# Graph network layer on one core: the forward transform of each 64-time tile as products of their own, instead of one product against a table with zeros

## The chip, the cores and the metric

One NeuronCore of one Trainium2 chip (eight cores) runs the whole kernel as one launch. The metric is the time of one execution on the device in microseconds. Lower is better.

## The reference, cut to what matters

There are 64 graphs of 256 nodes with 256 features, all in fp32. Two layers run one after the other, each as x + layer(relu(layernorm(x))). Layer 0 is a normalised adjacency product and a linear map. Layer 1 takes, for each graph, the 256 nodes also as a sequence of 256 times:

```python
xc = jnp.transpose(x, (0, 2, 1))
h = _bn(_conv1d(xc, conv1_w, 0), bn1_g, bn1_b, bn1_m, bn1_v)      # 256 -> 256, one tap
h = jax.nn.relu(h)
h = _bn(_conv1d(h, conv2_w, 8), bn2_g, bn2_b, bn2_m, bn2_v)       # 256 -> 256, 17 taps
x_conv = jnp.transpose(jax.nn.relu(h + xc), (0, 2, 1))
...
A = jnp.exp(-dist) * mask
x_nmp = jnp.einsum('bnm,bmd->bnd', A, msg)
x_in = jnp.concatenate([x_conv, x_nmp], axis=-1)
gi = x_in @ w_ih.T + b_ih
gh = x @ w_hh.T + b_hh
```

and a gated update (sigmoid, sigmoid, tanh) behind it. The change concerns the convolution with 17 taps, which the kernel does with discrete Fourier transforms.

## The kernel before, in words

The kernel has three stages. The **first stage** is a software pipeline over the 64 graphs, one turn per graph and eleven more turns to drain. Each engine has its own function (`first_scalar`, `first_vector`, `first_gpsimd`, `first_tensor`, `first_sync`) with a hand-written order of steps, and each step works on the graph that is some turns behind (`live(i, lag)` gives b = i - lag). Semaphores join the engines, and every engine executes its own list strictly in the order written. The **second stage** goes over 40 frequencies: 256x256 complex products of spectra and filter spectra. The filter spectra come from `filter_unit` (L706, lhsT of 119 rows and for the last part 68 rows). The **third stage** goes over pairs of graphs: the inverse transform (L1019) and the gates.

TensorE's turn in the first stage is, in the order of `first_tensor`: `out0` (12 products of 256 columns with split operands, through the helper `multiply` at L113), `nmp` (12 more), `agg` (L615: four fp32 products of 256 columns), `dist` (L624: two), `s` (6 through L113), the **forward transform** (L644), `cm1` and `cm0` (12 of 512 columns through L113), and four transposes (L663). An fp32 product with fp32 operands shows in the trace as two weight loads and two matmuls. A product with operands of the rounded type fp32r (all of L113, L624) shows as one of each.

The forward transform cuts the 256 times of a graph into four tiles of 64, zero-padded to NT = 80. Two tiles lie above each other on the 128 partitions of `h1[b % 2][:, n, :]`: tile t of half n on rows 64t to 64t + 63. The table `ft` is 128 x 160. Its rows 0 to 63 hold the 80 cosines and sines in columns 0 to 79 and zeros in the rest, and its rows 64 to 127 hold zeros in columns 0 to 79 and the same 80 in columns 80 to 159. So one product with all 128 rows gives both tiles' spectra side by side. Per graph there are four such products, for channel half c and node half n; c = 0 goes to PSUM bank `DFT`, c = 1 to bank `OUT0`, which the graph's `out0` also uses. That is why the c = 1 half waits for `u` (L641): VectorE's step at L473 reads `OUT0` in the same turn.

ScalarE copies each bank to the staging tile `xst` in `spectrum_out` (L324, called at L379 and L386 with the cast `axh`, L384, between the calls); it signals `xe0` and `xe1`. `store_spectra` (L277 to L283) sends each quarter of a group of four graphs out on SP's queue. Other steps that the text speaks of: ScalarE's `msh` (L345), which waits for `nmp` of TensorE, its `xt` (L408) and `xxh` (L339), with which its own turn ends and the next begins; VectorE's `xxl` (L439), which waits for `xxh`, then `uvh` (L444), `uv` (L448), `ah` (L458), and `u` (L473).

Of the kernel before, what the change touches and what calls it, by code (L numbers as in the profile page):

```python
# [14 lines left out]
NT = 80  # L15
NF = NT // 2
TILE = 64
# [83 lines left out]
def mm3(lhs, rhs, o, first, last, pairs):  # L101

    n = 3 * len(pairs)
    i = 0
    for l, r in pairs:
        for a, c in ((0, 0), (0, 1), (1, 0)):
            yield lhs[a][l], rhs[c][r], o, first and i == 0, last and i == n - 1
            i += 1


def multiply(e, steps):
    for l, r, o, start, stop in steps:
        done = e.matmul(o, l, r, start=start, stop=stop, skip_group_check=True)  # L113
    return done
# [14 lines left out]
def gnn_kernel(nc, x, adj, adjt, w0t, w1mt, wset, wgt, w2r, bc, cols, ftab, gtab, ttab, eye, out):  # L129
    NB = x.shape[0]  # L130
# [19 lines left out]
    with ExitStack() as ctx:  # L150
        S = {n: ctx.enter_context(nc.semaphore(n)) for n in NAMES}
        P = [ctx.enter_context(nc.psum_tensor(f"P{i}", [128, 512], F32)) for i in range(8)]
# [23 lines left out]
        ft = p1("ft", [128, 2 * NT])  # L176
# [40 lines left out]
        h1 = [p1(f"h1{i}", [128, 2, 256]) for i in range(2)]  # L217
        af = p1("af", [128, 512])
        xst = [p1(f"xst{i}", [128, 2, NT, 16]) for i in range(2)]
# [27 lines left out]
        DFT, OUT0, NMP, DIST, AG, SXN, CM1, CM0 = range(8)  # L247
# [11 lines left out]
        def live(i, lag, n=NB):  # L259
            return 0 <= i - lag < n  # L260
# [16 lines left out]
        def store_spectra(e, k):  # L277

            g, c, r = k // 4, k % 2, k % 4 // 2
            e.wait_ge(S[f"xe{c}"], 4 * g + 4)  # L280
            e.e.dma_start(xh_d[:, c, r * NF // 4:(r + 1) * NF // 4, g, :],
                          xst[g % 2][:, c, r * NF:(r + 1) * NF, :].rearrange("p (q s) t -> p q (s t)", s=4)).then_inc(
                              S[f"sx{'ab'[r]}{g % 2}"], 16)  # L283

        def first_sync(e, i):
            if live(i, 0):
                if i + 1 < NB:
                    load_x(e, i + 1)
                    load_adj(e, i + 1)
                load_adjt(e, i)  # L290

            if live(i, 11, NB - 4):
                store_spectra(e, i - 11)
            if NB + 7 <= i < NB + 9:
                for n in range(2):
                    store_spectra(e, NB - 4 + 2 * (i - NB - 7) + n)
            if live(i, 8):
                b = i - 8
                e.wait_ge(S["nm"], b + 1)
                e.e.dma_start(nm_d[b], nm[:, :]).then_inc(S["snm"], 16)  # L300
            if live(i, 4):
                b = i - 4
                e.wait_ge(S["x2"], b + 1)
                e.e.dma_start(x2_d[b].rearrange("(t p) c -> p t c", p=128), x2[b % 2][:, :, :]).then_inc(S[f"sx2{b % 2}"], 16)
            if live(i, 5):
                b = i - 5
                e.wait_ge(S["xt"], b + 1)
                e.e.dma_start(xn_d[b // 2][:, :, b % 2, :],
                              xt[:, :].rearrange("p (c t) -> p c t", c=2)).then_inc(S["sxt"], 16)
            if live(i, 8, NW):  # L310
                j = i - 8
                n = 17 * parts(j)
                e.wait_ge(S["taps"], j - 1)
                e.e.dma_start(taps[0:n, j, :], w2r[119 * j:119 * j + n]).then_inc(S[f"tap{j % 2}"], 16)

        def spectrum_out(e, b, c):

            g, j = b // 4, b % 4
            src = P[(DFT, OUT0)[c]][:, 0:4 * NT].rearrange("p (j r) -> p r j", j=4)
            dst = xst[g % 2][:, c, :, 4 * j:4 * j + 4]  # L320
            e.wait_ge(S[f"dft{c}"], b + 1)
            for half in "ab":
                e.wait_ge(S[f"sx{half}{g % 2}"], 32 * (g // 2))
            e.e.copy(dst, src).then_inc(S[f"xe{c}"], 1)  # L324

        def relu(e, b):
            e.wait_ge(S["tcm0"], b + 1)
# [4 lines left out]
        def first_scalar(e, i):  # L332
# [45 lines left out]
            if live(i, 7):  # L378
                spectrum_out(e, i - 7, 0)  # L379
# [5 lines left out]
            if live(i, 7):  # L385
                spectrum_out(e, i - 7, 1)  # L386
# [193 lines left out]
        def first_tensor(e, i):  # L580
            if live(i, 3):
                b = i - 3
# [5 lines left out]
                for n in range(2):  # L588
                    t = multiply(e.e, mm3([{f: h[:, f * 256 + n * 128:f * 256 + n * 128 + 128] for f in range(2)}
                                           for h in ag],  # L590
                                          [{f: h[:, f, :] for f in range(2)} for h in w0],
                                          P[OUT0][:, n * 256:n * 256 + 256], True, True, [(0, 0), (1, 1)]))
                t.then_inc(S["out0"], 1)
            if live(i, 7):
                b = i - 7
# [5 lines left out]
                for d in range(2):  # L601
                    t = multiply(e.e, mm3([{m: h[:, m, d * 128:d * 128 + 128] for m in range(2)} for h in ms],
                                          [{m: h[:, m * 256:m * 256 + 256] for m in range(2)} for h in ax],
                                          P[NMP][:, d * 256:d * 256 + 256], True, True, [(0, 0), (1, 1)]))
# [3 lines left out]
            if live(i, 2):  # L608
                b = i - 2
# [3 lines left out]
                for f in range(2):  # L613
                    for m in range(2):
                        t = e.e.matmul(P[AG][:, f * 256:f * 256 + 256], hd[b % 2][:, m, f * 128:f * 128 + 128],  # L615
                                       ah[b % 2][:, m * 256:m * 256 + 256], start=m == 0, stop=m == 1,
                                       skip_group_check=True)
                t.then_inc(S["agg"], 1)
            if live(i, 6):
                b = i - 6  # L620
                e.wait_ge(S["uv"], b + 1)
                e.wait_ge(S["af"], b)
                for m in range(2):
                    t = e.e.matmul(P[DIST][:, m * 256:m * 256 + 256], uv[0:96, 0, m * 128:m * 128 + 128],  # L624
                                   uv[0:96, 1, :], start=True, stop=True, skip_group_check=True)
                t.then_inc(S["dist"], 1)
            if live(i, 5):
                b = i - 5
# [6 lines left out]
            if live(i, 7):  # L635
                b = i - 7
                e.wait_ge(S["h1"], b + 1)
                e.wait_ge(S["ft_in"], 16)
                for c, k in ((0, DFT), (1, OUT0)):
                    if c == 1:  # L640
                        e.wait_ge(S["u"], min(b + 5, NB))  # L641
                    e.wait_ge(S[f"xe{c}"], b)
                    for n in range(2):
                        t = e.e.matmul(P[k][:, n * 2 * NT:n * 2 * NT + 2 * NT], h1[b % 2][:, n, c * 128:c * 128 + 128],  # L644
                                       ft[:, :], start=True, stop=True, skip_group_check=True)
                    t.then_inc(S[f"dft{c}"], 1)
            if live(i, 5):
                b = i - 5
                for k, n, name, freed in ((CM1, 1, "cm1", "tcm1"), (CM0, 0, "cm0", "tcm0")):
# [5 lines left out]
            if live(i, 4):  # L655
                b = i - 4
# [4 lines left out]
                for c in range(2):  # L661
                    for n in range(2):
                        t = e.e.transpose(P[SXN][:, c * 256 + n * 128:c * 256 + n * 128 + 128],  # L663
                                          xn[:, n, c * 128:c * 128 + 128], ident[:, :])
# [818 lines left out]
        def _(tensor):  # L1483
# [5 lines left out]
            for i in range(4):  # L1489
                first_tensor(e, i)  # L1490
# [5 lines left out]
            for n in range(2):  # L1496
                t = tensor.matmul(P[CM0][:, n * 128:n * 128 + 128], ones[:, :], diag[:, 4 + n, :],
                                  start=True, stop=True, skip_group_check=True)
            t.then_inc(S["rows"], 1)
            first_tensor(e, 4)  # L1500
            e.wait_ge(S["normrow"], 2)
            for i in range(5, TURNS):
                first_tensor(e, i)
# [62 lines left out]
```

## Time and profile before

| | |
|---|---|
| median of 3 runs | 1789.55 us (1788.72 to 1789.57) |
| profiled execution | 1790.36 us |
| its span, first to last instruction | 1788.6 us |
| TensorE's granted clock, mean over the span | 0.998 |
| first stage | about 0 to 660 us |

The profile is one execution, recorded by the hardware. "Busy" of TensorE is modelled from start times and sizes, so that the distance between two starts (the pitch) says more than a duration does. PE is TensorE's matmul side, PEld its weight loads, DVE VectorE, ACT ScalarE, POOL GpSimd, SP the engine that issues DMAs. A merged row ("x8") spans from the first start to the last end of that many equal instructions in a row.

### The profile page before, as it was taken

Reading aid. Unit: us, or ns where it says so; the run is one execution under the profiler, and the core shown is the slowest. Engines: PE = TensorE matmul, PEld = TensorE weight load, DVE = VectorE, ACT = ScalarE, POOL = GpSimd, SP = SyncE. Lnnn points to the kernel's source line nnn. Section 1 sums busy time; section 2 is a strip of 40 time slices with the busy share of each in tenths; the row PEclk is TensorE's granted clock in tenths of the full one; section 3 lists DMA queues with packets and bytes.
Section 4 is the critical chain, followed back from the end, with each engine's and each line's share of the span. In section 5 each row is a group of like instructions: output and inputs, shape, how many; then the busy total and the mean of one; then the engine's idle time right before and its main releaser. Section 6 shows DMA issues by size and latency. Waiting matters only on the chain.

```text
span 1788.6 us, 29955 instructions
## 1 busy us (share of the span) xinstructions
PE 1774.4 (99%) x10266; PEld 1574.9 (88%) x10266; DVE 1212.5 (68%) x2318; ACT 997.3 (56%) x1787; POOL 830.7 (46%) x991
## 2 busy tenths in 40 slices
PE   8999999999999999999999999999999999999998
PEld 7999999999999999999988888888888888888887
DVE  8999999999999847665664454554554544545545
ACT  5888888888888876665743233233332332332322
POOL 5788888887777627655722122221221221212211
PEclk9999999999999999999999999999999999999999
DMA  6566666676656554544762534534435345344342
GB/s 214 179 201 210 206 207 209 201 214 191 209 184 202 144 163 148 179 161 171 245 189 73 123 79 108 116 78 116 93 97 120 79 107 116 81 115 101 91 111 42
DMA packets 511381, 262.56 MB, mean 147 GB/s; under 512 B 366215, under 2 KB 474119, under 8 KB 511230
## 3 DMA queue, kind: packets, MB, share of 16 engines
q1 hardware_dynamic: 510686, 260.58, 52.3%
q8 instruction: 83, 1.36, 0.3%
q14 instruction: 68, 0.56, 0.1%
q10 hardware_dynamic: 544, 0.07, 0.0%
HBM read 151.51 MB, written 109.05 MB: 146 GB/s over the span
## 4 chain that ended last, share of the span: by engine, by line
PE 97%; issue 1%; POOL 1%; DVE 0%; ACT 0%; DMA 0%; SPq 0%; POOLq 0%; ACTq 0%; DVEq 0%
PE P L113 72%; PE P L615 6%; PE P L1019 5%; PE P L874 4%; PE P L644 4%; PE P L706 3%; PE P L663 1%; PE P L624 1%; PE P L1488 1%; DMA tt_w<-in_ttab 0%; POOL axl L578 0%; POOL af L575 0%; ACT xn L354 0%; DVE wh0l L837 0%; DVE x L473 0%
## 5 line engine op out<-in xcount | busy, mean ns | idle before, releaser
L1001 POOL TENSOR_TENSOR xnx1l<-xnf,xnx1h 128x1024 fp32r<-128x1024 f32 x16 | 44.2, 2761 | 336.2 <-ACT xnx1h L994 336.2
L1001 POOL TENSOR_TENSOR xnx0l<-xnf,xnx0h 128x1024 fp32r<-128x1024 f32 x15 | 41.6, 2774 | 317.1 <-ACT xnx0h L994 317.1
L1124 ACT ACTIVATE tr<-P,cold 128x512 f32<-128x512 f32 x64 | 44.2, 690 | 192.3 <-PE P L113 192.3
L1127 ACT ACTIVATE nn<-gn,col 128x512 f32<-128x512 f32 x64 | 46.4, 724 | 182.3 <-DVE gn L1148 182.3
L1157 DVE SCALAR_TENSOR_TENSOR tz<-tz,tr 128x512 f32<-128x512 f32 x63 | 43.6, 692 | 142.5 <-ACT tz L1138 142.5
L1138 ACT ACTIVATE tz<-P,cold 128x512 f32<-128x512 f32 x63 | 43.4, 688 | 156.8 <-PE P L113 156.8
L1144 DVE SCALAR_TENSOR_TENSOR gn<-tr,gn 128x512 f32<-128x512 f32 x64 | 45.0, 703 | 125.9 <-ACT tr L1124 125.9
L575 POOL TENSOR_TENSOR af<-af,at 128x512 f32<-128x512 f32 x64 | 110.1, 1720 | 42.8 <-ACT af L366 40.5
L578 POOL TENSOR_TENSOR axl<-af,axh 128x512 fp32r<-128x512 f32 x64 | 101.2, 1582 | 55.6 <-ACT axh L384 55.6
L615 PE MATMUL P<-ah,hd 128*128 128x256 f32 x512 | 121.4, 380 | 0.0
L113 PE MATMUL P<-w1mh,xxh 128*128 128x512 f32 x256 | 107.9, 422 | 0.0
L1019 PEld LDWEIGHTS P<-gt,yt 128*128 128x128 f32 x768 | 98.9, 190 | 4.9
L615 PEld LDWEIGHTS P<-ah,hd 128*128 128x128 f32 x512 | 93.2, 191 | 10.0
L113 PE MATMUL P<-w1mh,xxl 128*128 128x512 f32 x256 | 101.2, 395 | 0.0
L113 PE MATMUL P<-w1ml,xxh 128*128 128x512 f32 x256 | 101.1, 395 | 0.0
L1019 PE MATMUL P<-gt,yt 128*128 128x136 f32 (+1 forms) x768 | 100.8, 281 | 0.0
L498 DVE SCALAR_TENSOR_TENSOR x<-x,x 128x512 f32<-128x512 f32 x64 | 99.8, 1559 | 0.1
L899 DVE TENSOR_TENSOR yo<-P,mt 128x512 f32<-128x512 f32 x78 | 53.5, 686 | 66.5 <-PE P L113 66.5
L1148 DVE TENSOR_TENSOR gn<-gn,P 128x512 f32<-128x512 f32 x64 | 44.0, 688 | 66.9 <-PE P L113 66.9
L706 PE MATMUL P<-tt_w,taps 119*128 119x140 f32 (+1 forms) x592 | 80.8, 283 | 0.0
L113 PE MATMUL P<-w0h,agh 128*128 128x256 f32 x256 | 77.5, 303 | 3.2 <-DVE w0l L463 2.1
L726 ACT COPY wf<-P 128x420 f32<-128x420 f32 (+1 forms) x94 | 46.8, 512 | 60.1 <-PE P L706 59.9
(215 smaller groups left out, 6423.0 us busy)
## 6 DMA issues: line engine op xcount, KB each, us to landing
xh_d<-xst SPq DMA_DIRECT2D x64, 320.0 KB, 4.6
y_d<-yo SPq DMA_DIRECT2D x80, 256.0 KB, 2.2
xl<-xh_d SPq DMA_DIRECT2D x36, 512.0 KB, 4.5
x<-in_x SPq DMA_DIRECT2D x64, 256.0 KB, 2.7
a<-in_adj SPq DMA_DIRECT2D x64, 256.0 KB, 3.1
at<-in_adjt SPq DMA_DIRECT2D x64, 256.0 KB, 3.9
x_d<-x SPq DMA_DIRECT2D x64, 256.0 KB, 4.2
xn_d<-xt SPq DMA_DIRECT2D x64, 256.0 KB, 4.0
```

The lines of the kernel that those rows point to most:

```text
L113: done = e.matmul(o, l, r, start=start, stop=stop, skip_group_check=True)
L498: e.e.scalar_tensor_tensor(out=o[:, :, :], in0=o[:, :, :], scalar=0.0, in1=xs[b % 5][:, :, :], op0=ALU.max, op1=ALU.add).then_inc(S["x2"], 1)
L575: e.e.tensor_tensor(af[:, :], af[:, :], at[b % 7][:, :], ALU.mult).then_inc(S["am"], 1)
L578: e.e.tensor_tensor(ax[1][:, :], af[:, :], ax[0][:, :], ALU.subtract).then_inc(S["axlo"], 1)
L615: t = e.e.matmul(P[AG][:, f * 256:f * 256 + 256], hd[b % 2][:, m, f * 128:f * 128 + 128], ah[b % 2][:, m * 256:m * 256 + 256], start=m == ...
L644: t = e.e.matmul(P[k][:, n * 2 * NT:n * 2 * NT + 2 * NT], h1[b % 2][:, n, c * 128:c * 128 + 128], ft[:, :], start=True, stop=True, skip_gr ...
L706: t = e.e.matmul(P[k][:, m * 140:m * 140 + 140], taps[0:n_rows, j0 + m, c * 128:c * 128 + 128], tt_w[0:n_rows, part * 140:part * 140 + 140 ...
L726: e.e.copy(dst, src).then_inc(S["wev"], 1)
L874: t = e.e.matmul(common(chunk)[:, 0:256], xsum[f % 3][:, c, 128 * chunk:128 * chunk + 128], wsum[f % 3][:, c, :], start=c == 0, stop=c == ...
L899: e.e.tensor_tensor(yo[n % 4][:, :].rearrange("p (q o) -> p q o", q=2), main(chunk)[:, :].rearrange("p (q o) -> p q o", q=2), mt[chunk][:, ...
L1001: e.e.tensor_tensor(o[1][:, :, :], xnf[p % 2][:, :, :, :].rearrange("p c i t -> p c (i t)"), o[0][:, :, :], ALU.subtract).then_inc(done, 1)
L1019: t = e.e.matmul(P[k][:, o * 256 + first:o * 256 + end], y[:, j, o * 128:o * 128 + 128], gt[:, g:g + end - first], start=o == 0 and j == 0 ...
```

## The change

The transform is issued as eight products of 64 rows and 80 columns rather than four of 128 rows and 160 columns. Tile t reads rows 64t to 64t + 63 of `h1` and of `ft`, and writes to a bank that belongs to the tile (t = 0 to `DFT`, t = 1 to `OUT0`) where before the bank belonged to the channel half. The two tiles' products alternate. All waits (for `u`, for both `xe`) now stand ahead of the first product, and both banks are signalled at the end. `spectrum_out` and `store_spectra` follow: a copy takes one tile's spectra of both channel halves and writes every other element of four, and a store waits for both copies. The table `ft` is not changed.

```diff
         def store_spectra(e, k):
 
             g, c, r = k // 4, k % 2, k % 4 // 2
-            e.wait_ge(S[f"xe{c}"], 4 * g + 4)
+            for t in range(2):
+                e.wait_ge(S[f"xe{t}"], 4 * g + 4)
...
-        def spectrum_out(e, b, c):
+        def spectrum_out(e, b, t):
 
             g, j = b // 4, b % 4
-            src = P[(DFT, OUT0)[c]][:, 0:4 * NT].rearrange("p (j r) -> p r j", j=4)
-            dst = xst[g % 2][:, c, :, 4 * j:4 * j + 4]
-            e.wait_ge(S[f"dft{c}"], b + 1)
+            src = P[(DFT, OUT0)[t]][:, 0:4 * NT].rearrange("p (c n r) -> p c r n", c=2, n=2)
+            dst = xst[g % 2][:, :, :, 4 * j + t:4 * j + 4:2]
+            e.wait_ge(S[f"dft{t}"], b + 1)
             for half in "ab":
                 e.wait_ge(S[f"sx{half}{g % 2}"], 32 * (g // 2))
-            e.e.copy(dst, src).then_inc(S[f"xe{c}"], 1)
+            e.e.copy(dst, src).then_inc(S[f"xe{t}"], 1)
...
                 b = i - 7
                 e.wait_ge(S["h1"], b + 1)
                 e.wait_ge(S["ft_in"], 16)
-                for c, k in ((0, DFT), (1, OUT0)):
-                    if c == 1:
-                        e.wait_ge(S["u"], min(b + 5, NB))
-                    e.wait_ge(S[f"xe{c}"], b)
+                e.wait_ge(S["u"], min(b + 5, NB))
+
+                for t in range(2):
+                    e.wait_ge(S[f"xe{t}"], b)
+                for c in range(2):
                     for n in range(2):
-                        t = e.e.matmul(P[k][:, n * 2 * NT:n * 2 * NT + 2 * NT], h1[b % 2][:, n, c * 128:c * 128 + 128],
-                                       ft[:, :], start=True, stop=True, skip_group_check=True)
-                    t.then_inc(S[f"dft{c}"], 1)
+                        for t, k in ((0, DFT), (1, OUT0)):
+                            at_ = (2 * c + n) * NT
+                            rows = slice(TILE * t, TILE * t + TILE)
+                            d = e.e.matmul(P[k][:, at_:at_ + NT], h1[b % 2][rows, n, c * 128:c * 128 + 128],
+                                           ft[rows, NT * t:NT * t + NT], start=True, stop=True, skip_group_check=True)
+                            if c == 1 and n == 1:
+                                d.then_inc(S[f"dft{t}"], 1)
```

## Rows read from the trace of the kernel before

**Rows 1.** The page: busy time by engine, TensorE's clock, the chain that ended last.

```profile
PE 1774.4 (99%) x10266; PEld 1574.9 (88%) x10266; DVE 1212.5 (68%) x2318; ACT 997.3 (56%) x1787; POOL 830.7 (46%) x991
...
PEclk9999999999999999999999999999999999999999
...
PE 97%; issue 1%; POOL 1%; DVE 0%; ACT 0%; DMA 0%; SPq 0%; POOLq 0%; ACTq 0%; DVEq 0%
```

**Rows 2.** Windows, the steady first stage, one turn: us, then PE, PEld, DVE, ACT, POOL busy.

```profile
402.02:411.85 9.83, 9.83 (x67) 9.03 (x65) 9.57 (x24) 8.63 (x18) 7.99 (x14) 1.00 0.75 242
```

**Rows 3.** Timeline of PE in one turn: start us, us, engine, line, operation, out<-in, count.

```profile
400.27 0.28 PE L113 MATMUL P<-axh,msl 128*128 128x256 f32 x1
400.39 1.89 PE L615 MATMUL P<-ah,hd 128*128 128x256 f32 x8
...
402.94 0.28 PE L113 MATMUL P<-xxh,wsel 128*128 128x256 f32 x1
403.06 1.25 PE L644 MATMUL P<-ft,h 128*128 128x160 f32 x8
404.04 0.50 PE L113 MATMUL P<-w1mh,xxh 128*128 128x512 f32 x1
404.38 0.39 PE L113 MATMUL P<-w1ml,xxh 128*128 128x512 f32 x1
404.61 0.39 PE L113 MATMUL P<-w1mh,xxl 128*128 128x512 f32 x1
```

**Rows 4.** The line L644: durations in ns (min/median/max), first and last start.

```profile
L644 PE MATMUL P<-ft,h x512: 297/299/302, 49.2 to 659.8; 128*128 128x160 f32 x171
```

**Rows 5.** Timelines of PE and PEld, the shortest fp32 products (128 columns, ahead of the pipeline).

```profile
18.65 1.05 PE L1493 MATMUL P<-diag,ones 128*128 128x128 f32 x8
...
19.43 0.53 PEld L1497 LDWEIGHTS P<-diag,ones 128*128 128x128 f32 x4
```

**Rows 6.** Lines L1488 and L1497: 128 columns at the low clock and at the full one.

```profile
L1488 PEld LDWEIGHTS P<-ones x52: 191/333/337, 1.1 to 9.7; 128*128 128x128 f32 x52
L1488 PE MATMUL P<-ones x52: 274/421/584, 1.1 to 9.8; 128*128 128x128 f32 x52
...
L1497 PEld LDWEIGHTS P<-diag,ones x4: 192/192/193, 19.4 to 19.8; 128*128 128x128 f32 x4
L1497 PE MATMUL P<-diag,ones x4: 275/276/276, 19.5 to 19.9; 128*128 128x128 f32 x4
```

**Rows 7.** Groups by line and shape, weight loads of L706: count, busy us, mean ns.

```profile
L706 PEld LDWEIGHTS P<-tt_w,taps 119*128 119x128 f32 x576 | 73.4, 190 | 0.1
...
L706 PEld LDWEIGHTS P<-tt_w,taps 68*128 68x128 f32 x16 | 2.5, 192 | 0.0
```

**Rows 8.** Timeline of PEld, the transposes of one turn, and the line L663 in ns.

```profile
34.46 0.59 PEld L663 LDWEIGHTS P<-ident,xn 128*128 128x128 f32 x4
...
L663 PEld LDWEIGHTS P<-ident,xn x256: 137/141/144, 24.5 to 641.1; 128*128 128x128 f32 x128
```

**Rows 9.** Timelines of PEld and PE where TensorE starts again after a wait.

```profile
31.09 0.19 PEld L113 LDWEIGHTS P<-xxh,wseh 128*128 128x128 f32 x1 [2.11 <-ACT xxh L339]
...
31.32 0.28 PE L113 MATMUL P<-xxl,wseh 128*128 128x256 f32 x1
31.43 0.28 PE L113 MATMUL P<-xxh,wsel 128*128 128x256 f32 x1
```

**Rows 10.** Timelines of DVE and ACT in the turn of rows 3.

```profile
399.64 0.69 DVE L439 TENSOR_TENSOR xxl<-P,xxh 128x512 fp32r<-128x512 f32 x1 [0.21 <-ACT xxh L339]
...
402.09 0.87 DVE L473 SCALAR_TENSOR_TENSOR x<-P,sm,b 128x256 f32<-128x256 f32 x2
...
400.67 0.63 ACT L345 ACTIVATE msh<-tcm 128x512 fp32r<-128x512 f32 x1 [1.06 <-PE P L113]
...
404.93 0.43 ACT L324 COPY xst<-P 128x320 f32<-128x320 f32 x1
...
408.82 0.62 ACT L339 CAST xxh<-xt 128x512 fp32r<-128x512 f32 x1
```

**Rows 11.** Waits of SP's queue up to 700 us: us in total, times, longest.

```profile
SPq L98 <- DVE x L498: 189.5, 59, 6.5
...
SPq L281 <- ACT xst L324: 9.0, 3, 5.7
```

## The prediction

> **What bounds the kernel now.** First the page: TensorE is busy 99% of the span at the full clock, and 97% of the chain that ended last is its own work [rows 1]. So the question is which stretch the change touches and whether TensorE is dense there. The windows answer it: one turn of the first stage lasts 9.83 us, TensorE fills all of it, VectorE 9.57, ScalarE 8.63, GpSimd 7.99 [rows 2]. TensorE is the bound, and VectorE stands only 9.83 - 9.57 = 0.26 us behind it. Time added to TensorE's turn is added to the kernel 64 times; time taken from it comes back only as far as VectorE and the waits between the engines let it.
>
> The timeline gives the price of the transform now. Its eight matmuls span 1.25 us, the last lasting 0.299 [rows 3, 4], so the pitch is (1.25 - 0.30) / 7 = 0.136 us, and the block costs 8 x 0.136 = 1.09 us of a turn: from 403.06 to 404.15, where the next block's first product must have begun (404.38 less one pitch of 0.23). For 160 columns of fp32 that is near 2 cycles a column at 2.4 GHz, 0.133 us. This block is bound by the moving columns; its loads hide beneath them.
>
> **The change part by part.** It removes 8 matmuls of 160 columns and 8 loads a turn and issues 16 of each, with 80 columns. The moving columns are halved product by product: 0.136 / 2 = 0.068 us for each, 16 x 0.068 = 1.09 us, as much as before. Nothing is won by that unless the two halves of the array work at the same time.
>
> *The loads.* There are now twice as many, each still of 128 columns. Does a load of 64 rows cost less? L706 loads 68 rows in 192 ns and 119 rows in 190 [rows 7]: rows don't matter there. How short can the pitch of an fp32 load be? A load's record has a fixed part, but between the low clock (1.2 GHz) and the full one its median falls by 333 - 192 = 141 ns, and that of a matmul with 128 columns by 421 - 276 = 145 ns [rows 6]. So a load seems to occupy its path about as long as 128 moving columns occupy theirs. The pitch of such products is (1.05 - 0.275) / 7 = 0.111 us, that of their loads (0.53 - 0.192) / 3 = 0.113 us [rows 5]. I take 0.112. One after another, 16 loads cost 16 x 0.112 = 1.79 us, which is 0.70 us more than the 1.09 of now. Over 64 turns: +45 us. The bounds for this term: below, the loads hide (pitch 0.068, +0 us); above, the pitch of the transposes, (0.59 - 0.141) / 3 = 0.150 us [rows 8], with 0.141 for one load, the median of that line, thus 16 x 0.150 = 2.40, +84 us. I take 0.112, because it is of the same type and columns as the new loads.
>
> *Do the tiles overlap?* No row of this trace has products on part of the rows, so it can't say. The order within a pair speaks against it: each fp32 product is load, matmul, load, matmul on one tile, and the other tile's pair follows. In rows 3 and 5 loads and matmuls go in the order written, with a load one place ahead. If that order also holds between tiles, the four loads of a pair stay in a line, and nothing overlaps. That is my forecast.
>
> *The change of mode.* A turn goes from products of all rows to products of half, and back. No row shows the price of that. Below it is 0. Above: the next load may not start before the last matmul has left. Where TensorE starts after a wait, the load begins at 31.09 and the first matmul takes effect at 31.32 - 0.11 = 31.21 [rows 9]: 0.11 us that are hidden elsewhere. The last matmul's own tail, 0.28 - 0.12 = 0.16 us [rows 3], comes on top: 0.27 us a switch. I take 0.11 a switch, since a load that loses its cover is the least that a separation of the two kinds costs, 0.22 us a turn, 64 x 0.22 = +14 us; bounds 0 and +35. The Trainium skill, "TensorEngine Tiling (Array Packing)", Key Properties, says that changing the tiling mode drains TensorE, while staying in a mode and changing the tile doesn't. By that rule the switch would cost the tail too, +35 us in place of +14; no row here can show it.
>
> *The waits.* The wait for `u` moves from the middle of the block to its front. `u` ends at 402.96 [rows 10], and TensorE reaches the block at 402.94 with its load and at 403.06 with its matmul [rows 3]: on the edge. VectorE's chain to `u` hangs on `xxh` (402.96 is 3.32 behind the start of `xxl` at 399.64), and `xxh` on a ScalarE turn of 8.8 us that starts with `msh`, when TensorE's `nmp` is done [rows 10]. From that `nmp` to the next block TensorE has its whole turn with one transform in it. So if the transform grows, `u` is early by just that much and the wait costs nothing; queued behind it are `cm1`, `cm0`, the transposes and the next `out0`, none of which then waits. If it shrinks by g, `u` comes when it came, and the loop nmp, msh, xxh, u, transform, nmp covers two turns with only one transform shortened: half of g is given back.
>
> *The copies.* Both banks are signalled at the end of the block. ScalarE asks for the first at 404.93 [rows 10], 4.26 us behind `msh`. The old block's results are out at about 404.3. The new block ends 0.7 to 1.2 us later, so ScalarE stands still for up to 0.6 us. It has 1.06 us of idle time a turn, and the turn itself grows; `axh`, `h`, `nm`, `hd`, `xt` and `xxh` are queued behind it and slip by that much inside a longer turn. Cost 0. If the turn did not grow, this slip would reach `xxh` and `xxl`, which VectorE awaits already (0.21) [rows 10]. The copy keeps its 320 elements; bounds for the new stride are 0 and a copy twice as long, 2 x 0.43 us a turn, under ScalarE's 1.06; I take 0. SP's store waits for one semaphore more, but stores are issued a turn or more behind the copies, and SP spends 190 us waiting for `x2` anyway [rows 11]; cost 0, and at the end of the stage its wait is for the second copy already.
>
> **The sum.** 45 + 14 = +59 us. The profiled execution took 1790.36 us, 0.81 above the median of 1789.55; against it the changed kernel takes 1849.4, against the median 1848.6. I say **1849 us**. The forecast's own range is 1789.55 + 45 = 1835 to 1789.55 + 45 + 35 = 1870, with the slower load pitch a little more.
>
> **The rivals.** What a measurement can tell from no change is 0.2%, 3.6 us.
>
> *Both tiles work at once and the switch is cheap (ends faster).* Tile 1's loads and matmuls run beside tile 0's, so the block is eight steps of 0.112, the load still the slower part: 0.90 us, g = 0.19. The wait for `u` gives back half: 64 x 0.095 = 6 us, 1783. If the wait costs nothing, 64 x 0.19 = 12, 1777. It decides from the point at which the two switches together cost less than 0.19 us. For it: halves of different partitions share no rows. Against it: the order of the loads. The Trainium skill, "TensorE: Matmul & The Clock Gate", Part 3, says that products in distinct row groups run concurrently and that a load is pulled ahead when its row group differs from those in flight. This rival is what follows from it here.
>
> *Both at once, but each switch costs.* The block is 0.90 + 0.22 to 0.90 + 0.54 = 1.12 to 1.44 us, that is +2 to +22 us; middle +12, 1802.
>
> *Loads never bound, tiles in a line.* The block stays at 16 x 0.068 = 1.09 and the switches are free: 1790, the same. Against it stand the equal clock steps of rows 6.
>
> *Both at once and loads hidden as well.* Eight steps of 0.068 make 0.54, g = 0.55; half of it, 0.27, meets VectorE's 0.26: 64 x 0.26 = 17 us, 1773.
>
> **How the numbers follow.** Forecast 0.52, the pair with switch costs 0.18, the pair without 0.17, loads never bound 0.08, everything hidden 0.05. Faster: 0.17 + 0.05 = 0.22. Same: 0.08 + 0.02 of the second = 0.10. Slower: 0.52 + 0.16 = 0.68. For 8 in 10 the range must reach past 1783, the middle of the faster rival, and up to 1872; it leaves out the best case, half of the faster rival and a little above. It is wide since cases of both signs are open; the likeliest one's own range is 1835 to 1872.
>
> **What would show it.** In the changed trace L644's successor lines should have 16 records of each kind a turn, with starts 0.11 us apart, a block of about 2.0 us, and a turn of about 10.75 us with VectorE still at 9.6. Starts of the two tiles' matmuls within a few ns of each other would prove overlap and the forecast wrong. A block under 0.9 us with TensorE idle ahead of it, released by L473, would be the rival of the `u` wait. Gaps of over 0.1 us in front of and behind the block measure the switch. Behind 660 us nothing should change.

## The result and the profile after

The changed kernel takes 1799.91 us (median of 4 runs, 1799.2 to 1800.46) against 1789.56 us before: ratio 1.0058, 95% interval 1.0045 to 1.0071. It is 10.4 us slower. The prediction had the direction, but said 1849: its +59 us is nearly six times too much, so its account of the change was wrong. What came is one of its rivals: the two tiles work at the same time, and each change of mode is paid (+2 to +22 us, 1802, chance 0.18). A change of mode is here the step from products of all the rows to products of half of them, or back.

The windows of the changed kernel, for one steady turn; columns as in [rows 2]:

```profile
402.78:412.78 10.00, 10.00 (x75) 8.98 (x73) 9.58 (x24) 8.68 (x18) 7.87 (x14) 1.00 0.67 203
```

A turn takes 10.00 us in place of 9.83, TensorE still fills it, and the others have hardly changed. 64 x 0.17 = 10.9 us: the whole loss lies in these turns. The first and the last start of the transform say the same, 620.8 us apart (L649 below) in place of 610.6 [rows 4]. Behind the last transform the kernel before needs 1788.6 - 659.8 = 1128.8 us [rows 4] and the changed one 1797.9 - 668.9 = 1129.0.

TensorE's timeline in that turn, then the loads' (PEld), against [rows 3]:

```profile
407.70 0.27 PE L113 MATMUL P<-xxh,wsel 128*128 128x256 f32 x1
407.90 1.12 PE L649 MATMUL P<-ft,h 64*128 64x80 f32 x16
408.95 0.50 PE L113 MATMUL P<-w1mh,xxh 128*128 128x512 f32 x1
409.30 0.40 PE L113 MATMUL P<-w1ml,xxh 128*128 128x512 f32 x1
...
407.59 0.19 PEld L113 LDWEIGHTS P<-xxh,wsel 128*128 128x128 f32 x1
407.90 0.97 PEld L649 LDWEIGHTS P<-ft,h 64*128 64x128 f32 x16
408.95 0.19 PEld L113 LDWEIGHTS P<-w1mh,xxh 128*128 128x128 f32 x1
```

Sixteen matmuls span 1.12 us, less than the 1.25 us of the eight before. In a line at 0.112 us they would have spanned 15 x 0.112 + 0.27 = 1.95. They ran in twos. Cut to a short window, the timeline shows the first two loads together in 0.19 us, while the line's shortest load is 0.182 (third row below): the two starts are under 0.02 us apart. The first two matmuls together take 0.34, and the longest one of the line 0.334. In the trace's records the two tiles' starts are 6 to 7 ns apart.

```profile
407.90 0.19 PEld L649 LDWEIGHTS P<-ft,h 64*128 64x128 f32 x2
407.90 0.34 PE L649 MATMUL P<-ft,h 64*128 64x80 f32 x2
...
L649 PEld LDWEIGHTS P<-ft,h x1024: 182/188/188, 48.1 to 668.8; 64*128 64x128 f32 x171
L649 PE MATMUL P<-ft,h x1024: 272/272/334, 48.1 to 668.9; 64*128 64x80 f32 x171
```

The step between twos comes from the loads: (0.97 - 0.19) / 7 = 0.111 us. Eight steps are 0.89 us, 0.20 less than the old block's 1.09.

The block as a whole is nevertheless longer. By the prediction's own reckoning it lasts from 407.70 + 0.12 = 407.82 to 409.30 - 0.23 = 409.07, that is 1.25 us. So 1.25 - 0.89 = 0.36 us lie at its ends. In front, the first load starts 0.20 us behind the last matmul of the products before it (407.90 against 407.70). Behind, the last matmul starts at 409.02 - 0.27 = 408.75, and the next load at 408.95, again 0.20 us later. In the kernel before, load and matmul start together at both ends: at 402.94 in front (the matmul in [rows 3]), and behind at 404.01, where the last matmul starts at 403.06 + 1.25 - 0.30 = 404.01. Its loads:

```profile
402.94 1.12 PEld L644 LDWEIGHTS P<-ft,h 128*128 128x128 f32 x8
404.01 0.19 PEld L113 LDWEIGHTS P<-w1mh,xxh 128*128 128x128 f32 x1
```

The account that the experiments test is **+0.36 us a turn for two changes of mode, -0.20 for the overlap, 64 x 0.16 = +10.2 us**.

On the other engines, the chain that might have bound does not:

```profile
404.27 0.69 DVE L440 TENSOR_TENSOR xxl<-P,xxh 128x512 fp32r<-128x512 f32 x1 [0.38 <-ACT xxh L340]
...
406.72 0.87 DVE L474 SCALAR_TENSOR_TENSOR x<-P,sm,b 128x256 f32<-128x256 f32 x2
...
L325 ACT COPY xst<-P x128: 430/444/453, 49.8 to 669.5; 128x320 f32<-128x320 f32 x128
```

VectorE's idle time grows from 0.21 to 0.38 us. `u` ends at 407.59, 0.31 us ahead of the first load. The copies with the new stride take 444 ns (424 before), and all but two, in the last turns, find their bank ready.

### The profile page after: what moved, and what is told of

Same layout as the page of the kernel before. It is cut to its first block, busy times and chain, and to the rows that moved or that the text cites. A ratio compares the mean times of both kernels' runs of the same rounds, so it can differ in the third digit from the quotient of the medians.

```text
span 1797.9 us, 30995 instructions
## 1 busy us (share of the span) xinstructions
PE 1782.9 (99%) x10778; PEld 1568.7 (87%) x10778; DVE 1211.1 (67%) x2318; ACT 999.6 (56%) x1787; POOL 823.8 (46%) x991
## 4 chain that ended last, share of the span: by engine, by line
PE 96%; DVE 1%; issue 1%; POOL 1%; ACT 0%; DMA 0%; POOLq 0%; ACTq 0%; DVEq 0%
PE P L113 72%; PE P L616 6%; PE P L1025 5%; PE P L880 4%; PE P L649 4%; PE P L712 3%; PE P L669 1%; PE P L625 1%; POOL axl L579 0%; POOL af L576 0%; DMA x<-in_x 0%; DVE sm L487 0%; DVE sm L493 0%; DVE agl L421 0%; DVE x L474 0%
## 5 line engine op out<-in xcount | busy, mean ns | idle before, releaser
L576 POOL TENSOR_TENSOR af<-af,at 128x512 f32<-128x512 f32 x64 | 102.5, 1602 | 50.8 <-ACT af L367 50.7
L579 POOL TENSOR_TENSOR axl<-af,axh 128x512 fp32r<-128x512 f32 x64 | 92.1, 1439 | 64.7 <-ACT axh L385 64.7
L346 ACT ACTIVATE msh<-tcm 128x512 fp32r<-128x512 f32 x64 | 40.3, 630 | 77.5 <-PE P L113 77.0
```

Of the source, the lines that this page charges most:

```text
L576: e.e.tensor_tensor(af[:, :], af[:, :], at[b % 7][:, :], ALU.mult).then_inc(S["am"], 1)
L579: e.e.tensor_tensor(ax[1][:, :], af[:, :], ax[0][:, :], ALU.subtract).then_inc(S["axlo"], 1)
```

## The experiments

All ratios are to the kernel before, on the same chip. It took 1789.2 to 1789.5 us beside them and 1789.6 beside the changed kernel, so a difference to the changed kernel's 1799.91 holds to about 0.4 us.

### Is the gap in front a wait? (kernel before, waits moved)

```diff
+                e.wait_ge(S["u"], min(b + 5, NB))
+                for c in range(2):
+                    e.wait_ge(S[f"xe{c}"], b)
                 for c, k in ((0, DFT), (1, OUT0)):
-                    if c == 1:
-                        e.wait_ge(S["u"], min(b + 5, NB))
-                    e.wait_ge(S[f"xe{c}"], b)
```

> The kernel before, with the waits for u and both xe moved to the front of the transform, products unchanged. Theory A (the 10.4 us come from two changes of mode a turn, 0.15 us in front and 0.20 behind, less 0.19 gained by overlap): 1789.6 us, within 2 us of before. Rival B (the gap in front of the block is the moved wait for u, not the mode): 64 x 0.15 = +10 us, 1799.

Measured: 1792.38 us, ratio 1.0015 (1.0006 to 1.0024), +2.9 us. Theory A's bound of 2 us is missed by a little, rival B's +10 by far. The line's row shows what the edge costs:

```profile
L644 PE MATMUL P<-ft,h x512: 297/299/375, 48.6 to 661.8; 128*128 128x160 f32 x171
```

The first and last starts are 613.2 us apart, before 610.6 [rows 4]: 0.04 us a turn on the mean of 63, in which the load waits for `u`. The prediction had called this "on the edge". In the changed kernel the turn is 0.17 us longer, and `u` ends 0.11 us ahead of the last matmul in front of the block (407.59 against 407.70), so nothing of it remains there.

### What do the loads cost in a line? (changed kernel, all rows)

```diff
-                            d = e.e.matmul(P[k][:, at_:at_ + NT], h1[b % 2][rows, n, c * 128:c * 128 + 128],
-                                           ft[rows, NT * t:NT * t + NT], start=True, stop=True, skip_group_check=True)
+                            d = e.e.matmul(P[k][:, at_:at_ + NT], h1[b % 2][:, n, c * 128:c * 128 + 128],
+                                           ft[:, NT * t:NT * t + NT], start=True, stop=True, skip_group_check=True)
```

> The changed kernel, but each of the eight products of 80 columns uses all 128 rows (the zeros of the table take the other tile out), so there is no mode and no overlap. Theory A: 16 loads in a line at 0.112 us, no switch: 1.79 against 1.09 us a turn, +0.70 x 64 = +45 us over before, 1834. Rival C (loads of 128 columns take less than 0.068 us and hide; the 0.112 us steps of the changed kernel are something of the row tiles): 1790.

Measured: 1837.12 us, ratio 1.0265 (1.0249 to 1.0281), +47.6 us. Its transform, in the timeline of PE:

```profile
408.54 1.98 PE L649 MATMUL P<-ft,h 128*128 128x80 f32 x16
```

The pitch is (1.98 - 0.275) / 15 = 0.114 us. Rival C falls. The price of a load in the prediction was right, and this kernel is what the prediction took the changed one to be, without the modes: it costs the +45 us that stand there and 2.6 more.

The 2.6 come from `u`, nearly all. In every second turn (28 of 64) the first load waits for it and starts 0.14 us behind the matmul in front; in the others, with the same waits in the same place, load and matmul start together. So it is not the place of the waits that makes the gap of 0.20 us in the changed kernel. In one late turn `u` ends at 407.57 + 0.86 = 408.43 and the load starts at 408.50, where the matmul started at 408.36. The block's first matmul then starts at 408.54 in place of 408.36 + 0.12 = 408.48 and lasts 0.307 us in place of 0.275: 28 x 0.09 = 2.5 us. The lateness comes from an engine that bounds nothing: ScalarE's `axh` had waited 0.73 us for GpSimd's `af`, and `xxh`, `xxl` and `u` come after it.

```profile
401.00 0.62 ACT L385 CAST axh<-af 128x512 fp32r<-128x512 f32 x1 [0.73 <-POOL af L576]
...
407.57 0.86 DVE L474 SCALAR_TENSOR_TENSOR x<-P,sm,b 128x256 f32<-128x256 f32 x2
...
408.50 1.86 PEld L649 LDWEIGHTS P<-ft,h 128*128 128x128 f32 x16
```

### How far ahead are the tiles taken up? (tiles in a line, tiles by twos)

```diff
-                for c in range(2):
-                    for n in range(2):
-                        for t, k in ((0, DFT), (1, OUT0)):
+                for t, k in ((0, DFT), (1, OUT0)):
+                    for c in range(2):
+                        for n in range(2):
```

> The changed kernel with the loops exchanged: all four products of tile 0, then all four of tile 1. Theory A with a short look ahead (the overlap needs the tiles side by side in the program): 16 steps of 0.112 and two switches of 0.35 together, 2.14 against 1.09 us, +67 us over before, 1857. Rival D (the engine looks far enough ahead to take tile 1's loads and products while tile 0's run): 1800, as the changed kernel. Something between the two measures how far it looks.

Measured: 1831.21 us, ratio 1.0234 (1.022 to 1.0248), +41.7 us. It falls between the two theories. The loads in the timeline, whole and cut at 407.46:

```profile
406.93 1.48 PEld L649 LDWEIGHTS P<-ft,h 64*128 64x128 f32 x16
...
406.93 0.70 PEld L649 LDWEIGHTS P<-ft,h 64*128 64x128 f32 x6
```

All sixteen take (1.48 - 0.19) / 0.111 = 11.6 steps, where a line would take 15 and twos 7. Tile 0's first five loads start 0.11 us apart; the sixth of the second row starts at 0.70 - 0.18 = 0.52 us, ahead of the 0.55 at which tile 0's sixth is due. It is tile 1's first. When it starts, three of tile 0's eight are still to come. The records of the matmuls that carry the tiles' signals agree: tile 0's last starts at 407.78, tile 1's at 408.29, 0.51 us later, where the changed kernel has under 0.01 us between the two. So the engine takes up work of the free tile past loads and matmuls that wait for the busy one, in this order only some three of each far. The section on the kernel before says that every engine executes its list strictly in the order written. Between two tiles TensorE does not.

For the second order only the two inner loops are exchanged, so that the tile changes after every second product:

```diff
-                    for n in range(2):
-                        for t, k in ((0, DFT), (1, OUT0)):
+                    for t, k in ((0, DFT), (1, OUT0)):
+                        for n in range(2):
```

> The changed kernel with the tiles alternating after every second product (four loads and matmuls) rather than after every one. In the run with the tiles in line, tile 1's first load started beside tile 0's fifth matmul, with three left. Theory A with that look ahead (three loads and matmuls): tile 1 starts one or two steps of 0.112 late and the rest overlaps, +0.11 to 0.22 us a turn, +7 to +14 over the changed kernel, 1807 to 1814. Rival D (the look ahead counts more): 1800.

Measured: 1802.72 us, ratio 1.0076 (1.0059 to 1.0093), 2.8 us above the changed kernel. Between the theories again, and nearer to D: its sixteen loads span 1.03 us against 0.97, half a step late, not one or two. Four loads and matmuls of one tile in a row are nearly covered, eight are not.

```profile
409.62 1.03 PEld L649 LDWEIGHTS P<-ft,h 64*128 64x128 f32 x16
```

### What does a change of mode cost? (four changes, with a control)

```diff
                 for c in range(2):
+                    if c == 1 and live(i, 5):
+                        e.wait_ge(S["tcm1"], i - 5)
+                        multiply(e.e, cm_steps(1, CM1)[0:1])
                     for n in range(2):
```

This is the first product of `cm1`, which is left out behind the transform.

> The changed kernel with the first product of cm1 (all rows) moved into the middle of the transform, between channel halves, so that a turn has four changes of mode and the same work. Theory A: another 0.35 us a turn over 62 turns, +22 us over the changed kernel, 1822. Rival B (the gaps at the block's ends are waits, and a change of mode is free): 1800.

> Control for the run with four changes of mode: the same move of cm1's first product into the middle of the transform, made in the kernel before, where all products use all rows. Theory A: no mode, no cost, 1789 to 1791. If the move itself costs (the changed order, the wait for tcm1, the switch between fp32 and fp32r), up to the 21 us that it added to the changed kernel, 1810.

Measured: 1821.25 us with the changed kernel's products (ratio 1.0177, 1.0163 to 1.0191), which is 21.3 over the changed kernel, and 1789.63 us with those of the kernel before (1.0001, 0.9992 to 1.001). The same move costs nothing where all products use all rows, and 21.3 / 62 = 0.34 us a turn where it adds two changes of mode. Rival B falls. The timeline of PE with four changes:

```profile
400.15 0.27 PE L113 MATMUL P<-xxh,wsel 128*128 128x256 f32 x1
400.35 0.68 PE L657 MATMUL P<-ft,h 64*128 64x80 f32 x8
400.96 0.50 PE L113 MATMUL P<-w1mh,xxh 128*128 128x512 f32 x1
401.39 0.68 PE L657 MATMUL P<-ft,h 64*128 64x80 f32 x8
401.99 0.50 PE L113 MATMUL P<-w1ml,xxh 128*128 128x512 f32 x1
```

The 0.20 us between 400.15 and 400.35 is the gap in front that the changed kernel has, and there is one at each change (400.35 + 0.68 - 0.27 = 400.76 to 400.96, for one).

Fewer rows alone do not make the gap. `dist` uses 96 of the 128 rows, between products of all 128. In the kernel before its second matmul starts at 401.93 + 0.59 - 0.28 = 402.24, and so does the next load:

```profile
401.93 0.59 PE L624 MATMUL P<-uv 96*128 96x256 f32 x2
...
402.24 0.19 PEld L113 LDWEIGHTS P<-xxh,wseh 128*128 128x128 f32 x1
```

### Once a visit, or by the product? (one product split; the block three times)

In the kernel with the waits in front, one product of four is issued as two tiles, from the second graph on; its second half goes to the other bank, so these 80 spectra are stale.

```diff
                     for n in range(2):
+                        if c == 0 and n == 0 and b:
+                            for j, half_out in ((0, P[DFT]), (1, P[OUT0])):
+                                rows = slice(TILE * j, TILE * j + TILE)
+                                e.e.matmul(half_out[:, NT * j:NT * j + NT], h1[b % 2][rows, n, c * 128:c * 128 + 128],
+                                           ft[rows, NT * j:NT * j + NT], start=True, stop=True, skip_group_check=True)
+                            continue
```

> The kernel before with the waits in front (which took 1792.4), and one of its four products, the first, issued as the two 64-row products; its second tile goes to the other bank and is overwritten, so that part of the spectra is stale. Theory A: 0.35 us for the changes of mode, two steps of 0.112, three products of 0.272 left: 1.39 against 1.09 us, +0.30 x 63 = +19 over 1790, less what the moved wait costs, 1809. Rival G (a change of mode costs in proportion to the products in it): a quarter of the changed kernel's 10 us, 1793 to 1795.

Measured: 1807.96 us, ratio 1.0104 (1.0089 to 1.0119), +18.8 us. Splitting one product costs more than splitting all four: the change is paid once a visit, that is once for all the products between two changes of mode, and each split product earns a little back (two steps of 0.112 in place of 0.272 us). Rival G falls.

```profile
401.85 0.27 PE L113 MATMUL P<-xxh,wsel 128*128 128x256 f32 x1
402.05 0.45 PE L647 MATMUL P<-ft,h 64*128 64x80 f32 x4
402.43 1.08 PE L650 MATMUL P<-ft,h 128*128 128x160 f32 x6
```

Then the whole block three times in one visit, and as its measure the same in the kernel before:

```diff
-                for c in range(2):
+                for c in (0, 1, 0, 1, 0, 1):
...
-                    for n in range(2):
+                    for n in (0, 1, 0, 1, 0, 1):
```

The first of the two edits is to the changed kernel, where both banks are signalled after the last pair; the second is to the kernel before.

> The changed kernel with its whole block of products issued three times in a row (the same values to the same places), in one visit to the mode. Theory A: sixteen more steps of 0.112 us a turn, 1.79 x 64 = +115 us over the changed kernel, 1915. If the ends of the block cost in proportion to its products rather than once a visit: three times the block of 1.25 us, +160 us, 1960.

> The kernel before with its four products issued three times. Both theories: sixteen more steps of 0.136 us, 2.17 x 64 = +139 us, 1928. Theory A then has the run with the changed kernel's block three times 13 to 14 us below this one: with enough products in one visit the tiles win. If the ends cost in proportion, this one stays the faster by about 31 us.

Measured: 1913.84 us (1.0695, 1.0678 to 1.0713) and 1927.44 us (1.077, 1.0754 to 1.0787). The tiles now win by 13.6 us, as theory A has it: 64 x (0.36 - 3 x 0.20) = -15 us by the rounded terms. The loads of the one and the matmuls of the other:

```profile
401.48 2.76 PEld L650 LDWEIGHTS P<-ft,h 64*128 64x128 f32 x48
```

```profile
407.90 3.42 PE L644 MATMUL P<-ft,h 128*128 128x160 f32 x24
```

24 steps of (2.76 - 0.19) / 23 = 0.112 us stand against 24 of (3.42 - 0.30) / 23 = 0.136.

### What sets the step? (wider products, one tile)

```diff
-                            at_ = (2 * c + n) * NT
+                            at_ = (2 * c + n) * 128
...
-                            ... P[k][:, at_:at_ + NT] ... ft[rows, NT * t:NT * t + NT]
+                            ... P[k][:, at_:at_ + 128] ... ft[rows, 32 * t:32 * t + 128]
```

The 48 columns more are zeros of the table, and ScalarE's copy (`spectrum_out`) still takes the 80 that count.

> The changed kernel with 128 moving columns a product instead of 80 (the 48 more are zeros of the table, and land in unused columns of the banks). Theory A (the step of 0.112 us is the weight load's, and the moving columns hide below it as long as 2 cycles a column stay under it, 128 x 2 / 2.4 = 0.107 us): 1800, as the changed kernel, within 3 us. Rival E (the moving columns count in the step, or the end of the block): 8 x 0.04 us a turn, +20 us, 1820.

Measured: 1802.35 us, ratio 1.0073 (1.0058 to 1.0088), 2.4 us above the changed kernel. The loads take what they took:

```profile
409.29 0.97 PEld L649 LDWEIGHTS P<-ft,h 64*128 64x128 f32 x16
```

With 48 columns more the step stays at 0.111 us, so the load sets it. 2.4 / 64 = 0.04 us a turn is what 48 columns cost once (48 x 0.136 / 160 = 0.04): the sixteen matmuls span 1.16 us in place of 1.12. Rival E charged this in all eight steps and was right for one.

```profile
409.30 1.16 PE L649 MATMUL P<-ft,h 64*128 64x128 f32 x16
```

Last, three of tile 1's four products are left out (most of its spectra stay stale):

```diff
-                        for t, k in ((0, DFT), (1, OUT0)):
+                        for t, k in ((0, DFT), (1, OUT0))[0:2 if c == 1 and n == 1 else 1]:
```

> The changed kernel with three of tile 1's four products left out, so that most of the second tile's spectra are stale. Theory A (the second tile runs wholly beside the first and costs nothing): the same block, 1800, within 2 us. Rival F (the two tiles share something, for one the path of the loads): less by up to the three products' share, 6 x 0.056 us a turn, -21 us, 1779.

Measured: 1799.58 us, ratio 1.0057 (1.0042 to 1.0072), 0.3 us under the changed kernel. Its ten loads take 0.96 us, the sixteen of the changed kernel 0.97:

```profile
408.02 0.96 PEld L649 LDWEIGHTS P<-ft,h 64*128 64x128 f32 x10
```

The second tile costs nothing, loads included. Rival F falls.

## Why the prediction was wrong

*What bounds the kernel*: right. The loss is TensorE's turn, 64 times, and the time behind the last transform is the same within 0.2 us.

*The loads' price*: right in itself. 0.112 us was taken from products of the same kind; 0.114 was measured in a line, 0.111 in pairs. That rows don't matter was right too. The upper bound of 0.150 was misread: in the trace the four loads of [rows 8] start at 34.46, 34.70, 34.80 and 34.91, so one of them waits behind a matmul of 512 columns, and the others are 0.11 us apart. The forecast did not use it.

*"Do the tiles overlap?"*: this step failed, and with it the +45 us. The prediction argued from the order written, since loads and matmuls kept it everywhere in the trace. But no product of that trace fits on half of the rows. ("No row has products on part of the rows" is not exact: `dist` uses 96 rows, `filter_unit` 119 and 68.) So the order could not show what happens when two products need different halves. In the changed kernel tile 1's load and matmul start under 0.01 us after tile 0's; with the tiles in a line tile 1's first ones still start ahead of three of tile 0's. The term is -0.20 x 64 = -13 us instead of +45. The prediction said itself that the trace can't say, and then bounded the term for the loads by 0 and +84 us, both on one side of what came.

*The change of mode*: the mechanism was right, the size was not. The sum took 0.22 us a turn, the least; measured are 0.36 in the changed kernel and 0.34 for two further changes, +22 to +23 us in place of +14, inside the bounds of 0 to 0.54 us. In both directions the next load starts 0.20 us behind the last matmul's start, rather than with it. The Trainium skill, "TensorEngine Tiling (Array Packing)", Key Properties, has it that a change of tiling mode drains TensorE and that tiles run their loads and matmuls in parallel; the runs agree with both, at 0.34 to 0.36 us a visit and at no cost for the second tile.

*The wait for `u`*: in the changed kernel it costs nothing, as predicted, and 0.04 us a turn where the turn keeps its length. But "if the transform grows, `u` is early by just that much" does not hold: in the run with all rows the turn is 0.7 us longer, and `u` is late in every second turn, for about 2.5 us in all. *The copies and the stores*: 0, as predicted; the copy grew by 20 ns.

*The rival* that came true gave the block 1.12 to 1.44 us; it is 1.25. Its chance of 0.18 was too low for a case that only the one unsupported step kept from being the forecast.

No run that does the whole work is faster than the kernel before. Splitting one product in place of four loses more, and by these terms a visit earns its 0.36 us back from about 0.36 / 0.20 x 4 = 7 split products on; one and four lose, twelve win. The block has four. Two graphs in one visit would have eight, for which the terms give 64 x (0.18 - 0.20) = -1 us, less than can be measured; their spectra would also need 640 columns a tile where a bank holds 512. No run shows it.

## What to carry to other kernels

Two products of half the rows, side by side on the two halves of the array, take the steps of one. Against one product that is padded with zeros, the gain is then only the shorter step, here 0.111 in place of 0.136 us. From it goes a fixed charge for each visit, here 0.36 us, so count the products between two changes of mode before splitting any. The step of 0.11 us is the weight load of 128 fp32 columns, whether 80 or 128 columns move, so moving fewer columns than 128 shortens no step. Where a trace holds no case of a thing, the order that it shows elsewhere is no evidence against it: give both ends their weight.

## What the hardware showed that was not expected

- With 64-row products the second tile is free, loads too: ten loads take 0.96 us, sixteen take 0.97.
- The work of a free tile is taken up past waiting loads and matmuls, but only about three of each far. Alternating the tiles at every product gives 7 steps between the first load and the last, at every second product 7.6, tiles in a line 11.6 (15 without any overlap).
- A change between all rows and half the rows puts 0.20 us between a matmul's start and the next load's, in both directions; a pair of changes costs 0.34 to 0.36 us. Products of 96 rows between products of 128 make no such gap.
- GpSimd, 1.84 us short of filling a turn [rows 2], still makes `u` late in every second turn of the run with all rows.
